# Causal attention with three score slots in place of four, and a PSUM bank of its own for turned reciprocals and weighted sums

## The chip, the cores and the metric

The kernel runs on one core of a Trainium2 chip. The metric is the device time of one execution in microseconds (us): from before the first instruction to after the last. Engines are named as the profile names them: PE is TensorE (matrix multiplies, PEld its weight loads), DVE is VectorE, ACT is ScalarE, POOL is GpSimd, SP is SyncE, which here only issues DMAs. Each has its own instruction stream and runs it in order; they meet at semaphores. PSUM is the small memory that PE writes and DVE and ACT read. The program allots it in eight banks of 512 float32 columns.

## The reference, cut to what matters

The program is a stack of four blocks (cross attention, windowed attention with feed forward, cross attention, experts). The change touches only the first attention of the first block, which is a self attention of 2 batches, 1024 tokens, 16 heads of 32 channels:

```python
q = jnp.einsum('bsc,hcd->bhsd', xn, wq)
k = jnp.einsum('btc,hcd->bhtd', yn, wk)
v = jnp.einsum('btc,hcd->bhtd', yn, wv)
a = jax.nn.softmax(jnp.einsum('bhsd,bhtd->bhst', q, k) * D ** (-0.5), axis=-1)
if causal:
    s, t = (a.shape[-2], a.shape[-1])
    mask = (jnp.arange(t)[None, :] > jnp.arange(s)[:, None]).astype(a.dtype)
    a = a * mask
o = jnp.einsum('bhst,bhtd->bhsd', a, v)
```

The mask keeps keys later than the query and is applied after the softmax. So the softmax runs over all 1024 keys, and only the blocks on and above the diagonal are weighted with the values.

## The kernel before

The work is cut in units. A unit is 128 query rows of one head against all 1024 keys; there are 256. Four heads make a quad, and the units run quad by quad (8 quads), in a quad by block of 128 queries (8 tiles), in a tile by head (4 units). `place(n)` gives the quad, the tile within it and the head of unit n. The number of key blocks that a unit keeps is `blocks(n)`: 8 in the first tile of a quad, 7 in the second, down to 1 in the last. This text calls it T, and a tile "T=7" when its units keep 7 blocks. One quad is thus 32 units.

A unit goes through six steps, each a function of the source:

- `score(n)` on PE: two matmuls of 512 columns write the 1024 scores into a slot, two PSUM banks, one a half.
- `row_max(n)` on DVE: the negated row maximum over the whole slot.
- `exponent(n)` on ACT: the exponential of the whole slot into `prob`, with the row sum.
- `turn(n)` on PE: T transposes of 128x128 from `prob` back into the same slot. With T above 4 they lie in both halves, else in half 0 alone.
- `evacuate(n)` on DVE and ACT: copies of the turned blocks to `probT`. `evac_parts(n)` deals them: with T=8 DVE takes half 0 and ACT half 1, with T=7 to 5 ACT takes half 0 and DVE half 1, with T of 4 and less one engine takes all, DVE for even heads and ACT for odd.
- POOL masks the diagonal block.

Once per tile, after its four units: `inverse` (DVE, reciprocals of the row sums), a broadcast on POOL, `turn_inverses` (PE, one transpose), `inverses` (ACT, copy to `rT`), `weigh` (PE, 4T matmuls with a column group each, shown by the profile as 8T instructions), and `output` (DVE, the product of the weighted sums with `rT`).

Nothing but the order in which these calls are written sets the order of the work. PE's is `turn(n)`, then once per tile `turn_inverses` and `weigh`, then `score(n + 3)`. DVE's is `row_max(n + 2)`, `evacuate(n)`, and once per tile `output`. ACT's is `exponent(n + 1)`, `evacuate(n)`, and once per tile `inverses`. The slots rotate: unit n uses slot n % 4, so `score(n + 3)` writes the slot of unit n - 1 and waits for that unit's evacuation, each half for the part that lies in it. Four slots fill all eight banks, so the turned reciprocals and the weighted sums of a tile have to borrow a slot (`home` says which), and the score that comes next into that slot waits for `rT` or for `output`.

The functions and lines that the change and the prediction touch:

## Time and profile before

| | us |
|---|---|
| median of 3 runs | 2074.62 (2074.13 to 2076.19) |
| span of the profiled execution, first to last instruction | 2082.0 |
| PE, DVE, ACT, POOL busy over the span | 1797.5, 1276.7, 1038.0, 698.8 |
| this attention: first score to last output | 109.4 to 564.1 |
| granted TensorE clock, mean over the span | 0.953 |

The profiled execution has no time of its own apart from its span; the span is 7.4 us above the median of the runs. Busy shares are means over the whole program. What one stage waits for is read from rows of that stage. A row of the timeline gives start, duration, engine, line and what it writes and reads, and in brackets how long the engine had been idle and which instruction ended that.

### The profile page before, as it was taken

Reading aid. Unit: us, or ns where it says so; the run is one execution under the profiler, and the core shown is the slowest. Engines: PE = TensorE matmul, PEld = TensorE weight load, DVE = VectorE, ACT = ScalarE, POOL = GpSimd, SP = SyncE. Lnnn points to the kernel's source line nnn. Section 1 sums busy time; section 2 is a strip of 40 time slices with the busy share of each in tenths; the row PEclk is TensorE's granted clock in tenths of the full one; section 3 lists DMA queues with packets and bytes.
Section 4 is the critical chain, followed back from the end, with each engine's and each line's share of the span. In section 5 each row is a group of like instructions: output and inputs, shape, how many; then the busy total and the mean of one; then the engine's idle time right before and its main releaser. Section 6 shows DMA issues by size and latency. Waiting matters only on the chain. (4 is left out here: it accounts for less than half of the span.)

```text
span 2082.0 us, 32325 instructions
## 1 busy us (share of the span) xinstructions
PE 1797.5 (86%) x11428; PEld 1190.9 (57%) x11428; DVE 1276.7 (61%) x2721; ACT 1038.0 (50%) x2198; POOL 698.8 (34%) x1001
## 2 busy tenths in 40 slices
PE   6988888888799897998899989999998998871895
PEld 3455555555566565766566655556666554550795
DVE  5478888898733485233788863258888344977112
ACT  3488888888722264121676741147675211540222
POOL 0022223232333343242465641125565112450322
PEclk9999999999999998999999999999999999995898
DMA  3441111110000100020000002010000000046595
GB/s 117 157 129 42 42 42 42 42 42 1 1 1 0 54 8 1 0 62 26 19 6 5 3 6 66 0 44 1 6 6 6 20 0 16 1 135 152 173 309 168
DMA packets 104896, 101.71 MB, mean 49 GB/s; under 512 B 34896, under 2 KB 88480, under 8 KB 104608
## 3 DMA queue, kind: packets, MB, share of 16 engines
q1 hardware_dynamic: 101664, 95.31, 15.4%
q0 software_dynamic: 3072, 4.34, 1.1%
q8 instruction: 92, 1.51, 0.3%
q14 instruction: 68, 0.56, 0.1%
HBM read 80.60 MB, written 16.92 MB: 47 GB/s over the span
## 5 line engine op out<-in xcount | busy, mean ns | idle before, releaser
L586 DVE TENSOR_REDUCE negmax<-sps 128x1 f32<-128x1024 f32 x256 | 308.3, 1215 | 36.4 <-PE sps L531 31.1
L630 ACT ACTIVATE prob<-sps,negmax 128x1024 f32<-128x1024 f32 x256 | 287.6, 1124 | 22.1 <-DVE negmax L586 18.3
L540 PE MATMUL sps<-ident,prob 128*128 128x128 f32 x1152 | 177.6, 282 | 57.6 <-ACT prob L630 56.6
L540 PEld LDWEIGHTS sps<-ident,prob 128*128 128x128 f32 x1152 | 134.0, 143 | 142.5 <-ACT prob L630 123.3
L1504 POOL TENSOR_TENSOR la_pr<-la_pr,la_ri 128x512 f32<-128x512 f32 x128 | 157.3, 1257 | 159.5 <-DVE la_ri L1567 159.5
L675 POOL TENSOR_TENSOR probT<-probT,after 128x128 f32<-128x128 f32 x256 | 117.0, 457 | 267.8 <-DVE probT L594 192.2
L1754 ACT ACTIVATE la_pr<-la_pr,la_nx 128x256 f32<-128x256 f32 x256 | 126.4, 494 | 127.4 <-DVE la_nx L1608 127.4
L531 PE MATMUL sps<-ks,qs 128*128 128x512 f16 x512 | 162.6, 393 | 10.6 <-DVE ores L606 4.4
L1939 PE MATMUL la_bs<-lf_zT,lfw 128*128 128x512 f32 x352 | 153.0, 594 | 0.0
L1514 POOL TENSOR_TENSOR la_qs<-la_qn,ores 128x256 f32<-128x256 f32 x128 | 113.9, 921 | 89.3 <-DVE la_qn L1621 89.3
L639 ACT COPY probT<-sps 128x512 f32<-128x512 f32 (+1 forms) x192 | 101.9, 531 | 40.4 <-PE sps L540 40.4
L1939 PEld LDWEIGHTS la_bs<-lf_zT,lfw 128*128 128x128 f32 x352 | 66.4, 190 | 82.5 <-issue 82.3
L1881 PE MATMUL la_bqk<-ores,la_hT 128*128 128x512 f32 x224 | 104.3, 608 | 0.0
L1948 PE MATMUL la_bqk<-lfw,lf_hT 128*128 128x256 f32 (+1 forms) x384 | 95.4, 392 | 2.3 <-DVE lf_hT L1664 2.3
L1608 DVE CUSTOM_DVE_ANT_0 la_pr<-la_bs,la_mf 128x256 f32<-128x256 f32 x256 | 90.7, 419 | 10.6 <-PE la_bs L1898 10.5
L1664 DVE SCALAR_TENSOR_TENSOR lf_hT<-la_bs,lfb,lf_gl 128x512 f32<-128x512 f32 (+1 forms) x48 | 35.9, 749 | 94.8 <-ACT lf_gl L1782 92.8
L1782 ACT ACTIVATE lf_gl<-la_bs,lfb 128x512 f32<-128x512 f32 x40 | 27.5, 687 | 132.2 <-PE la_bs L1939 132.2
L1824 PE MATMUL la_bs<-ident,la_pr 128*128 128x128 f32 x512 | 74.0, 292 | 22.2 <-POOL la_pr L1504 22.2
L594 DVE COPY probT<-sps 128x512 f32<-128x512 f32 (+3 forms) x192 | 91.7, 478 | 1.3 <-PE sps L540 1.3
L1824 PEld LDWEIGHTS la_bs<-ident,la_pr 128*128 128x128 f32 x512 | 61.6, 149 | 46.8 <-POOL la_pr L1504 34.3
L1948 PEld LDWEIGHTS la_bqk<-lfw,lf_hT 128*128 128x128 f32 (+1 forms) x384 | 68.3, 189 | 29.8 <-issue 18.4
L563 PE MATMUL sps<-probT,vres 128*32 128x128 f32 x2304 | 78.7, 281 | 0.3 <-POOL probT L675 0.3
(375 smaller groups left out, 3742.3 us busy)
## 6 DMA issues: line engine op xcount, KB each, us to landing
w1e<-in_fc_T SPq DMA_DIRECT2D x16, 1024.0 KB, 5.7
w2e<-in_fc_T SPq DMA_DIRECT2D x16, 1024.0 KB, 8.9
qs<-q_parts SPq DMA_DIRECT2D x128, 64.0 KB, 1.9
ks<-k_parts SPq DMA_DIRECT2D x128, 64.0 KB, 1.9
q_parts<-parts SPq DMA_DIRECT2D x8, 512.0 KB, 3.6
k_parts<-parts SPq DMA_DIRECT2D x8, 512.0 KB, 3.6
lfw<-in_L_ffn_w SPq DMA_DIRECT2D x6, 640.0 KB
ores<-in_L_ffn_wqkv SPq DMA_DIRECT2D x2, 1536.0 KB, 6.5
```

Source lines behind the costliest of these rows:

```text
L531: mm = pe.matmul(slots[n % 4][:, half * 512:(half + 1) * 512], qs[:, buf, i * P:(i + 1) * P], ks[:, buf, half * 512:(half + 1) * 512], sta ...
L540: mm = pe.transpose(slots[n % 4][:, at * P:(at + 1) * P], prob[:, n % 3, t * P:(t + 1) * P], ident[:])
L586: dve.tensor_reduce(negmax[:, n % 4:n % 4 + 1], slots[n % 4][:], X, ALU.max, negate=True).then_inc(s.max_done, 1)
L630: act.activation(prob[:, n % 3, :], slots[n % 4][:], ACT.Exp, bias=negmax[:, n % 4:n % 4 + 1], accum_out=rowsum[:, tile % 2, n % QUAD:n % ...
L675: pool.tensor_tensor(blk, blk, after[:], ALU.mult).then_inc(s.masked, 1)
L1504: ins = pool.tensor_tensor(prob[:, h:h + 2, :], prob[:, h:h + 2, :], rinv[:, h:h + 2].unsqueeze(2).to_broadcast([P, 2, 2 * P]), ALU.mult)
L1514: pool.tensor_tensor(qs[:, q * HL:(q + 1) * HL, a * 32:(a + 1) * 32], qn[:, q * HL:(q + 1) * HL, (1 - a) * 32:(2 - a) * 32], sinr[:, t % T ...
L1754: ins = act.activation(prob[:, h, :], prob[:, h, :], ACT.Exp, scale=-1.0, bias=nmax[:, h:h + 1], accum_out=rsum[:, h:h + 1])
L1824: mm = pe.transpose(bs[:, half * 1024 + n * 256 + w * P:half * 1024 + n * 256 + (w + 1) * P], prob[:, h, w * P:(w + 1) * P], ident[:])
L1881: mm = pe.matmul(raw(t)[:, n * INNER:(n + 1) * INNER], shifted_rows(t, k), wqkv[:, k, n, :], start=(k == 0), stop=(k == KD - 1))
L1939: mm = pe.matmul(dst, w1[:, k, at:at + P], zT[:, k, :], start=(k == 0), stop=(k == KD - 1))
L1948: mm = pe.matmul(p3[j // 2][:, j % 2, :], uT[0:n, f, j * P:(j + 1) * P], w2[0:n, f, :], start=(f == 0), stop=(f == NF - 1))
```

## The change

PSUM is divided anew: three score slots (six banks) and one bank `wps`, whose first 128 columns take the turned reciprocals and whose second 128 the weighted sums. One bank stays free. `home` and the waits that went with the borrowed slot are gone. On PE, `score` now runs two units ahead and stands in front of `turn(n)`; `turn_inverses` comes ahead of `turn` too; and `weigh` comes one unit later, ahead of that unit's `turn`. `output` on DVE is one unit later. On ACT, `inverses` goes ahead of `evacuate`. `row_max(n + 2)` ahead of `evacuate(n)` on DVE stays as it was. Unit n now uses slot n % 3, so `score(n + 2)` writes the slot of unit n - 1.

PE before, from unit 2 to unit 7; `sps` with its number is a slot, x8 are eight transposes, and the number of blocks tells the tile:

```order
L540 MATMUL sps2<-ident,prob 128x128 x8
L531 MATMUL sps1<-ks,qs 128x512 x2
L540 MATMUL sps3<-ident,prob 128x128 x8
L531 MATMUL sps2<-ks,qs 128x512 x2
L540 MATMUL sps0<-ident,prob 128x128 x7
L547 MATMUL sps3<-ident,rwide 128x128
L563 MATMUL sps3<-probT,vres 32x128 x32
L531 MATMUL sps3<-ks,qs 128x512 x2
L540 MATMUL sps1<-ident,prob 128x128 x7
L531 MATMUL sps0<-ks,qs 128x512 x2
L540 MATMUL sps2<-ident,prob 128x128 x7
L531 MATMUL sps1<-ks,qs 128x512 x2
```

PE after the change, at the same place (line 524 is `score`, 533 `turn`, 540 `turn_inverses`, 556 `weigh`):

```order
L524 MATMUL sps1<-ks,qs 128x512 x2
L533 MATMUL sps2<-ident,prob 128x128 x8
L524 MATMUL sps2<-ks,qs 128x512 x2
L533 MATMUL sps0<-ident,prob 128x128 x8
L524 MATMUL sps0<-ks,qs 128x512 x2
L540 MATMUL wps<-ident,rwide 128x128
L533 MATMUL sps1<-ident,prob 128x128 x7
L524 MATMUL sps1<-ks,qs 128x512 x2
L556 MATMUL wps<-probT,vres 32x128 x32
L533 MATMUL sps2<-ident,prob 128x128 x7
L524 MATMUL sps2<-ks,qs 128x512 x2
L533 MATMUL sps0<-ident,prob 128x128 x7
```

The score that refills the slot of unit n - 1 stood behind `turn(n)`; it stands ahead of it now. `weigh` stood between a `turn` and a `score`; it stands between a `score` and a `turn`.

DVE before, the same units (586 is `row_max`, 594 `evacuate`, 600 `inverse`, 606 `output`):

```order
L594 COPY probT<-sps1 128x512
L586 TENSOR_REDUCE negmax<-sps0 128x1
L594 COPY probT<-sps2 128x512
L586 TENSOR_REDUCE negmax<-sps1 128x1
L600 RECIPROCAL rinv<-rowsum 128x4
L594 COPY probT<-sps3 128x512
L586 TENSOR_REDUCE negmax<-sps2 128x1
L594 COPY probT<-sps0 128x384
L606 TENSOR_TENSOR ores<-sps3,rT 128x128
L586 TENSOR_REDUCE negmax<-sps3 128x1
```

DVE after the change (580 `row_max`, 588 `evacuate`, 594 `inverse`, 600 `output`):

```order
L588 COPY probT<-sps1 128x512
L580 TENSOR_REDUCE negmax<-sps1 128x1
L588 COPY probT<-sps2 128x512
L580 TENSOR_REDUCE negmax<-sps2 128x1
L594 RECIPROCAL rinv<-rowsum 128x4
L588 COPY probT<-sps0 128x512
L580 TENSOR_REDUCE negmax<-sps0 128x1
L588 COPY probT<-sps1 128x384
L580 TENSOR_REDUCE negmax<-sps1 128x1
L588 COPY probT<-sps2 128x384
```

The order of kinds is the same but for `output`. The slots differ: before, the copy out of one slot was followed by the maximum of another that had been filled a unit earlier; now it is followed by the maximum of the very slot that was just copied out.

The diff, cut to its core:

```diff
@@ -470,7 +470,9 @@
             rT = sb("rT", [P, 2, P], F32, c)
-            slots = [ps(f"sps{i}", [P, N], c) for i in range(4)]
+            NS = 3
+            slots = [ps(f"sps{i}", [P, N], c) for i in range(NS)]
+            wps = ps("wps", [P, 2, P], c)
 
             def place(n):
@@ -491,11 +493,6 @@
             def evacuated(who, n):
 
                 return sum(part[0] == who for m in range(n + 1) for part in evac_parts(m))
-
-            def home(tile):
-
-                nxt = tile * QUAD + QUAD
-                return 0 if nxt < UNITS and blocks(nxt) <= 4 else QUAD - 1
 
             s = signals("a1a", "@cleared @after_ready @scores @max_done @exp_done @masked "
                         "@turned @evac_act @evac_dve @rinv_done @widened @r_turned @rT_done @pv_done @out_done @next_in")
@@ -518,17 +515,13 @@
                         if i == 0:
                             pe.wait_ge(landed[buf], 128 * (quad // 2 + 1))
                         for half in range(2):
-                            if n >= 4:
-                                for who, lo, _ in evac_parts(n - 4):
+                            if n >= NS:
+                                if half == 0:
+                                    pe.wait_ge(s.exp_done, n - NS + 1)
+                                for who, lo, _ in evac_parts(n - NS):
                                     if lo // 4 == half:
-                                        pe.wait_ge(s.evac_act if who == "act" else s.evac_dve, evacuated(who, n - 4))
-                            if half == 0 and j == QUAD - 1 and n > QUAD:
-                                pe.wait_ge(s.rT_done, n // QUAD)
-                            if half == 1 and j == QUAD - 1 and n > QUAD and home(n // QUAD - 1) == QUAD - 1:
-                                pe.wait_ge(s.out_done, n // QUAD)
-                            if half == 1 and j == 0 and n > QUAD and home(n // QUAD - 2) == 0:
-                                pe.wait_ge(s.out_done, n // QUAD - 1)
-                            mm = pe.matmul(slots[n % 4][:, half * 512:(half + 1) * 512], qs[:, buf, i * P:(i + 1) * P],
+                                        pe.wait_ge(s.evac_act if who == "act" else s.evac_dve, evacuated(who, n - NS))
+                            mm = pe.matmul(slots[n % NS][:, half * 512:(half + 1) * 512], qs[:, buf, i * P:(i + 1) * P],
                                            ks[:, buf, half * 512:(half + 1) * 512], start=True, stop=True)
                         mm.then_inc(s.scores, 1)
@@ -537,21 +530,21 @@
                         pe.wait_ge(s.exp_done, n + 1)
                         for at in range(total):
                             t = i + 1 + at if at < total - 1 else i
-                            mm = pe.transpose(slots[n % 4][:, at * P:(at + 1) * P], prob[:, n % 3, t * P:(t + 1) * P], ident[:])
+                            mm = pe.transpose(slots[n % NS][:, at * P:(at + 1) * P], prob[:, n % 3, t * P:(t + 1) * P], ident[:])
                         mm.then_inc(s.turned, 1)
 
                     def turn_inverses(tile):
-                        who, last = evac_parts(tile * QUAD + QUAD - 1)[0][0], tile * QUAD + QUAD - 1
-                        pe.wait_ge(s.evac_act if who == "act" else s.evac_dve, evacuated(who, last))
+                        if tile > 0:
+                            pe.wait_ge(s.out_done, tile)
                         pe.wait_ge(s.widened, tile + 1)
-                        pe.transpose(slots[QUAD - 1][:, 0:P], rwide[:, tile % 2, :, :].rearrange("p h d -> p (h d)"),
+                        pe.transpose(wps[:, 0, :], rwide[:, tile % 2, :, :].rearrange("p h d -> p (h d)"),
                                      ident[:]).then_inc(s.r_turned, 1)
 
                     def weigh(tile):
                         last = tile * QUAD + QUAD - 1
                         quad, i, _ = place(last)
                         total = blocks(last)
-                        acc = slots[home(tile)]
+                        pe.wait_ge(s.rT_done, tile + 1)
                         for who, sem in (("act", s.evac_act), ("dve", s.evac_dve)):
                             if evacuated(who, last):
                                 pe.wait_ge(sem, evacuated(who, last))
@@ -560,20 +553,21 @@
                             if t == i:
                                 pe.wait_ge(s.masked, last + 1)
                             for j in range(QUAD):
-                                mm = pe.matmul(acc[j * D1:(j + 1) * D1, 512:512 + P], vres[:, quad * QUAD + j, t, :],
+                                mm = pe.matmul(wps[j * D1:(j + 1) * D1, 1, :], vres[:, quad * QUAD + j, t, :],
                                                probT[:, (tile * QUAD + j) % 6, at * P:(at + 1) * P],
                                                start=(at == 0), stop=(at == total - 1))
                         mm.then_inc(s.pv_done, 1)
 
-                    for n in range(3):
+                    for n in range(2):
                         score(n)
                     for n in range(UNITS):
-                        turn(n)
+                        if n + 2 < UNITS:
+                            score(n + 2)
                         if n % QUAD == 0 and n > 0:
                             turn_inverses(n // QUAD - 1)
+                        if n % QUAD == 1 and n > QUAD:
                             weigh(n // QUAD - 1)
-                        if n + 3 < UNITS:
-                            score(n + 3)
+                        turn(n)
                     turn_inverses(UNITS // QUAD - 1)
                     weigh(UNITS // QUAD - 1)
...
@@ -603,7 +597,7 @@
                         quad, i, _ = place(tile * QUAD)
                         dve.wait_ge(s.pv_done, tile + 1)
                         dve.wait_ge(s.rT_done, tile + 1)
-                        dve.tensor_tensor(ores[:, quad, i * P:(i + 1) * P], slots[home(tile)][:, 512:512 + P], rT[:, tile % 2, :],
+                        dve.tensor_tensor(ores[:, quad, i * P:(i + 1) * P], wps[:, 1, :], rT[:, tile % 2, :],
                                           ALU.mult).then_inc(s.out_done, 1)
 
                     row_max(0)
@@ -614,7 +608,7 @@
                         if n % QUAD == QUAD - 1:
                             inverse(n // QUAD)
                         evacuate(n)
-                        if n % QUAD == 0 and n > 0:
+                        if n % QUAD == 1 and n > QUAD:
                             output(n // QUAD - 1)
                     output(UNITS // QUAD - 1)
...
@@ -636,21 +630,21 @@
                                 act.wait_ge(s.turned, n + 1)
                                 if n >= 6:
                                     act.wait_ge(s.pv_done, (n - 6) // QUAD + 1)
-                                act.copy(probT[:, n % 6, lo * P:hi * P], slots[n % 4][:, lo * P:hi * P]).then_inc(s.evac_act, 1)
+                                act.copy(probT[:, n % 6, lo * P:hi * P], slots[n % NS][:, lo * P:hi * P]).then_inc(s.evac_act, 1)
 
                     def inverses(tile):
                         act.wait_ge(s.r_turned, tile + 1)
                         if tile >= 2:
                             act.wait_ge(s.out_done, tile - 1)
-                        act.copy(rT[:, tile % 2, :], slots[QUAD - 1][:, 0:P]).then_inc(s.rT_done, 1)
+                        act.copy(rT[:, tile % 2, :], wps[:, 0, :]).then_inc(s.rT_done, 1)
 
                     exponent(0)
                     for n in range(UNITS):
                         if n + 1 < UNITS:
                             exponent(n + 1)
-                        evacuate(n)
                         if n % QUAD == 0 and n > 0:
                             inverses(n // QUAD - 1)
+                        evacuate(n)
                     inverses(UNITS // QUAD - 1)
 
                 @block.gpsimd
```

Left out are three places where `slots[n % 4]` became `slots[n % NS]` and nothing else.

## Rows read from the trace of the kernel before

**Rows 1.** Windows, this attention: length, busy of PE, PEld, DVE, ACT, POOL, clock, DMA.

```profile
109.00:563.00 454.00, 375.86 (x4024) 241.18 (x4024) 394.85 (x575) 391.54 (x768) 134.24 (x322) 0.97 0.16 43
```

**Rows 2.** Groups of this attention by form: busy us, mean ns | idle before, releasers.

```profile
L586 DVE TENSOR_REDUCE negmax<-sps 128x1 f32<-128x1024 f32 x256 | 308.3, 1215 | 36.4 <-PE sps L531 31.1 <-ACT prob L630 5.2
L630 ACT ACTIVATE prob<-sps,negmax 128x1024 f32<-128x1024 f32 x256 | 287.6, 1124 | 22.1 <-DVE negmax L586 18.3 <-PE sps L540 1.8
...
L639 ACT COPY probT<-sps 128x512 f32<-128x512 f32 x144 | 84.2, 585 | 34.5 <-PE sps L540 34.5
...
L594 DVE COPY probT<-sps 128x512 f32<-128x512 f32 x48 | 32.5, 678 | 1.3 <-PE sps L540 1.3
L594 DVE COPY probT<-sps 128x384 f32<-128x384 f32 x48 | 26.1, 544 | 0.0
...
L594 DVE COPY probT<-sps 128x256 f32<-128x256 f32 x48 | 19.7, 411 | 0.0
...
L594 DVE COPY probT<-sps 128x128 f32<-128x128 f32 x48 | 13.3, 277 | 0.0
...
L639 ACT COPY probT<-sps 128x384 f32<-128x384 f32 x16 | 7.6, 474 | 2.3 <-PE sps L540 2.3
L639 ACT COPY probT<-sps 128x256 f32<-128x256 f32 x16 | 5.9, 368 | 1.2 <-PE sps L540 1.2
L639 ACT COPY probT<-sps 128x128 f32<-128x128 f32 x16 | 4.2, 264 | 2.3 <-PE sps L540 2.3
```

**Rows 3.** Timeline of all engines, first units of a T=7 tile: start, us, instruction.

```profile
233.72 1.95 PE L563 MATMUL sps<-probT,vres 128*32 128x128 f32 x64
...
235.60 0.39 PE L531 MATMUL sps<-ks,qs 128*128 128x512 f16 x1
235.74 0.29 DVE L606 TENSOR_TENSOR ores<-sps,rT 128x128 f32<-128x128 f32 x1 [0.74 <-PE sps L563]
...
236.18 0.38 PE L531 MATMUL sps<-ks,qs 128*128 128x512 f16 x1 [0.18 <-DVE ores L606]
...
236.39 0.93 PE L540 MATMUL sps<-ident,prob 128*128 128x128 f32 x7
236.59 1.23 DVE L586 TENSOR_REDUCE negmax<-sps 128x1 f32<-128x1024 f32 x1 [0.56 <-PE sps L531]
...
237.15 0.59 PE L531 MATMUL sps<-ks,qs 128*128 128x512 f16 x2
237.35 0.59 ACT L639 COPY probT<-sps 128x512 f32<-128x512 f32 x1 [1.58 <-PE sps L540]
...
237.58 0.93 PE L540 MATMUL sps<-ident,prob 128*128 128x128 f32 x7
...
238.19 1.22 DVE L586 TENSOR_REDUCE negmax<-sps 128x1 f32<-128x1024 f32 x1
...
239.32 0.55 DVE L594 COPY probT<-sps 128x384 f32<-128x384 f32 x1
...
239.79 1.22 DVE L586 TENSOR_REDUCE negmax<-sps 128x1 f32<-128x1024 f32 x1
```

**Rows 4.** Timeline of PE, where a tile T=4 is weighed and T=3 turned.

```profile
263.49 1.08 PE L563 MATMUL sps<-probT,vres 128*32 128x128 f32 x32
264.50 0.61 PE L531 MATMUL sps<-ks,qs 128*128 128x512 f16 x2
264.94 0.49 PE L540 MATMUL sps<-ident,prob 128*128 128x128 f32 x3
```

**Rows 5.** Line 547, once per tile: durations in ns, first and last start in us.

```profile
L547 PE MATMUL sps<-ident,rwide x64: 272/300/448, 120.1 to 562.4; 128*128 128x128 f32 x64
```

**Rows 6.** Windows of PE at a fall of the clock: length, busy, clock, DMA.

```profile
277.00:279.00 2.00, 2.00 (x7) 0.50 0.05 11
```

**Rows 7.** Timeline of PE in that stretch.

```profile
276.94 1.04 PE L531 MATMUL sps<-ks,qs 128*128 128x512 f16 x2
277.77 0.42 PE L540 MATMUL sps<-ident,prob 128*128 128x128 f32 x1
```

More of the change, by code:

```diff
@@ L585, in row_max @@
                             dve.wait_ge(s.exp_done, n - 3)
-                        dve.tensor_reduce(negmax[:, n % 4:n % 4 + 1], slots[n % 4][:], X, ALU.max, negate=True).then_inc(s.max_done, 1)
+                        dve.tensor_reduce(negmax[:, n % 4:n % 4 + 1], slots[n % NS][:], X, ALU.max, negate=True).then_inc(s.max_done, 1)
                     def evacuate(n):
@@ L593, in evacuate @@
                                     dve.wait_ge(s.pv_done, (n - 6) // QUAD + 1)
-                                dve.tensor_copy(probT[:, n % 6, lo * P:hi * P], slots[n % 4][:, lo * P:hi * P]).then_inc(s.evac_dve, 1)
+                                dve.tensor_copy(probT[:, n % 6, lo * P:hi * P], slots[n % NS][:, lo * P:hi * P]).then_inc(s.evac_dve, 1)
                     def inverse(tile):
@@ L629, in exponent @@
                             act.wait_ge(s.rinv_done, tile - 1)
-                        act.activation(prob[:, n % 3, :], slots[n % 4][:], ACT.Exp, bias=negmax[:, n % 4:n % 4 + 1],
+                        act.activation(prob[:, n % 3, :], slots[n % NS][:], ACT.Exp, bias=negmax[:, n % 4:n % 4 + 1],
                                        accum_out=rowsum[:, tile % 2, n % QUAD:n % QUAD + 1]).then_inc(s.exp_done, 1)
```

## The prediction, on record before the changed kernel ran

> **What bounds the stage now.** I read the windows of the stage first, then its groups, then the timeline of a few units. Over 454 us PE, DVE and ACT were busy 83, 87 and 86% [rows 1], so none alone is the answer. The groups show whole-slot passes: a row maximum of 1215 ns and an exponential of 1124 ns for each unit, then copies of 264 to 678 ns [rows 2]. The timeline shows two regimes. Inside a tile DVE is never idle: maximum at 238.19, copy at 239.32 (1.13 later), next maximum at 239.79, a period of 1.60 us [rows 3]. Once per tile the chain breaks: `weigh` holds PE from 233.72 to 235.60, the score behind it waits for `output`, and DVE idles 0.74 and 0.56 us and ACT 1.58 us [rows 3]. Line 547 runs once per tile, from 120.1 to 562.4 over 63 intervals [rows 5]: 7.02 us a tile, 56.2 us a quad of eight tiles.
>
> **What the row of 236.59 says.** In those 0.56 us DVE waited for a score whose second half waited for DVE's own product: the product ends at 236.03, the matmul starts at 236.18 (0.15), takes 0.38, and the maximum starts 0.03 after its end [rows 3]. That is the price of asking PE to refill a slot that DVE has only just left, and then waiting for it. Before, it is paid once per tile.
>
> **What the change adds.** `score(n+2)` needs unit n-1 evacuated. DVE does `evacuate(n-1)`, then `row_max(n+2)`, which reads that score, and only then `evacuate(n)`. So the 0.56 us is now in every unit, and in series with both DVE passes. Before, `score(n+3)` needed the same evacuation, but DVE's next maximum was that of n+2, already scored: one unit of slack. That slack is gone, and no engine has work to put there, since `turn(n)` too stands behind the score on PE. A count of slots alone would hide this: the loop through one slot (refill, maximum, exponential, turn, copy, with handovers) is about 0.15+0.38+0.03+1.22+0.03+1.12+0.15+0.93+0.03+0.55, some 4.6 us for three units, under the old 1.60 each [rows 2, 3].
>
> Period of a unit after the change, in us, from rows at full clock:
> - T=7, 6, 5 (DVE copies half 1): 0.56 + 1.13 + copy 0.55, 0.41, 0.28 [rows 2, 3] = 2.24, 2.10, 1.97. ACT, which copies half 0, ends earlier: with T=7 the turn is issued 0.21 after the score's second half, which begins 0.41 before the maximum, and ends 0.73 after the maximum's start; ACT's copy ends at 1.34, and it may be 1.47 (DVE's copy ends at 1.68, and half 0 wants 0.21 ahead of half 1). So a later turn shows from 0.13 us on (0.10 and 0.08 for T=6 and 5).
> - T=8 (DVE copies half 0): both score matmuls follow, 0.59 in place of 0.38 [rows 3]: 0.15 + 0.59 + 0.03 + 1.13 + 0.68 = 2.58. The turn ends at 0.84 and is wanted at 1.10, so it has 0.26 of slack.
> - T=4 to 1, two units together, since DVE copies the even one and ACT the odd: maximum 1.13, DVE copy, 0.15, score issue 0.43 (237.15 to 237.58), turn, 0.03, ACT copy, 0.15 + 0.59 + 0.03 to the next maximum [rows 3]. A turn of 7 blocks takes 0.93 and of 3 0.49 [rows 3, 4], so 0.11 a block, and 0.60, 0.38, 0.27 for 4, 2, 1. With the copies of [rows 2]: 4.37, 4.02, 3.66. With T=1 the exponential is later than the turn: 1.22 + 0.03 + 1.12 + 0.26 + 0.77 = 3.40.
>
> Four units a tile, T=8 down to 1: 10.32 + 8.96 + 8.40 + 7.88 + 8.74 + 8.04 + 7.32 + 6.80 = 66.5 us a quad.
>
> **Once per tile.** `weigh` holds PE 1.88 us for 64 instructions and 1.01 for 32 (263.49 to 264.50) [rows 3, 4]; between them on a line: 1.66, 1.45, 1.23, 0.79, 0.58, 0.36 for 56, 48, 40, 24, 16, 8. It now delays `turn(4k+1)`, and with it the copy, the next score and the next maximum, less the slack above. The tile of T units pays for T+1 blocks: T=7 1.75, T=6 1.56, T=5 1.37, T=4 1.23, T=3 1.01, T=2 0.79, T=1 0.50, T=8 0.10; sum 8.3. The serial part of the old boundary, PE's, is thus not removed but moved. What does go are the waits for the borrowed slot. `output` now fits into DVE's 0.56 us and costs nothing; if that cover went it would cost 0.2 a tile. The reciprocal ahead of a copy and the transposed reciprocals (0.30, [rows 5]) ahead of a turn add an estimated 0.7 a quad. ACT's copy of them ends during the turn: nothing. `turn_inverses`' wait for `output` and `weigh`'s for `rT` are for work ended a unit earlier or more. SP's loads wait for scores two quads back and have a longer quad to land in: nothing.
>
> **Sum.** 66.5 + 8.3 + 0.7 = 75.5 us a quad against 56.2; times 63/8 quads, +152 us.
>
> **The clock.** PE will be less busy, so its clock matters. From 277 to 279 it was at 1.2 GHz, half [rows 6]; a score pair took 1.04 there in place of 0.59, a turn of one block 0.42 in place of 0.27 [rows 7]. It fell in the lightest tiles, where PE had little to do in a unit. The stage's mean of 0.97 [rows 1] is 6% of it at 1.2 GHz, 3.4 us a quad: one fall of some two units a quad. For a pair of T=1 units at the low level the turn's path decides: 1.13+0.28+0.15+0.86+0.42+0.03+0.26+0.15+1.04+0.03 = 4.35, +0.95 over 3.40. The price is 0 if the falls stay as many, and +9.4 a quad if all tiles of T=4 to 1 run so (2.7, 2.5, 2.3 and 1.9 by the same path, with 0.22 a block), +75 in all. I take three falls a quad where there was one, two more of two units each: +15, nearer the low end since that is where the rows are.
>
> The Trainium skill has a rule that speaks against this change ("TensorE: Matmul & The Clock Gate", "A second HAM failure mode: psum-queue depth-cycling"): small idle gaps between groups of matmuls, repeated with each turn of the PSUM banks, make the clock swing between its levels. The rows bear it out only at the light tiles. By it the sum would be that of rival A.
>
> The profiled execution spans 2082.0, 7.4 above the median of the runs; differences carry over. 2074.6 + 152 + 15 = **2242 us** (its profile 2249).
>
> **Rivals.**
> - A, the low clock over all light tiles: 2074.6 + 152 + 75 = 2302. For it: PE now waits for a slot in every unit and is busy 0.43 + 0.60 us of 2.19 with T=4, 0.43 + 0.27 of 1.70 with T=1. Against: at the low level the same work fills more of the time, as the full 2.00 of 2.00 us of [rows 6] shows, and the clock came back after it. Chance 0.09.
> - B, half of the new wait is hidden: some order that I read as serial overlaps, say because PE's loss to `weigh` is caught up inside the tile. Half of 152: 2151, with 2100 to 2200 as its own range. Against: every link is an in-order engine. Chance 0.07; 0.01 of it for no change at all, if DVE's maximum did not wait and the loop of 4.6 us per three units were the only bound.
> - C, the other side: the borrowed slot was the real cost, and its own bank frees DVE's 0.74 + 0.56 us per tile: 63 x 1.30 = 82, so 1993. For it: these waits [rows 3], and the 31.1 us that the maxima waited for scores [rows 2]. It decides if `score(n+2)` is complete before DVE ends `evacuate(n)`; that takes a slot free a unit earlier, which three slots don't give. Chance 0.03.
> - The sum as above: 0.81.
>
> So faster by over 0.2% (about what a measurement of this kernel tells from none) 0.03, within it 0.01, slower 0.96. The range, 2195 to 2305, holds the sum with clock costs from 0 to 75 us, below that an error of 0.03 us in each unit's handover (8 us) or of three or four us a quad in `weigh`.
>
> **What would show it.** In the profile after: DVE idle of about 0.56 us before nearly each maximum in T=7 to 5 and 0.77 in the others, released by the score line, some 145 us in all where it was 31; maxima 2.24 us apart with T=7 and 2.58 with T=8; ACT's busy share of the stage down from 86 to about 65%; the stage some 605 us long; everything behind it unchanged. If idle before the maximum stays near 36 us, the serial chain is wrong; if the spacing holds but the stage is longer, the clock is the rest. If maxima in T=7 stay 1.6 us apart, the forecast is wrong altogether.

## The result, and the profile after

| | before | after |
|---|---|---|
| median, us | 2075.4 (4 runs) | 2306.12 (2298.2 to 2313.94, 4 runs) |
| span of the profiled execution, us | 2082.0 | 2296.4 |
| first to last row maximum of this attention, us | 448.8 | 678.7 |
| granted clock, mean of the span | 0.953 | 0.913 |

The ratio is 1.1094 (95% interval 1.1046 to 1.1142): slower, as forecast, but by 231 us where 167 were forecast. By the medians the time lies 64 us above the forecast and 1 us above the top of the range; by the ratio (1.1094 of 2075.4 is 2302) it lies just inside it.

It is in this attention: between its first and last row maximum 229.9 us came on. The medians are 230.7 apart; that these two agree so closely is partly luck. Behind the last maximum, where the instructions are the same, the profile of before took 1522.8 us and that of after 1507.4. The two spans are therefore only 214.4 apart. This stretch moves by some 15 us without any change: e1, below, took 1522.6 in it and e11 1507.4. Line 586 of before and line 580 of after are the same instruction (columns: line, engine, operation, tile, count: shortest/median/longest ns, first and last start in us; the last field is the shape of the commonest form):

```profile
L586 DVE TENSOR_REDUCE negmax<-sps x256: 1192/1215/1227, 110.4 to 559.2; 128x1 f32<-128x1024 f32 x128
```
```profile
L580 DVE TENSOR_REDUCE negmax<-sps x256: 1212/1224/1226, 110.3 to 789.0; 128x1 f32<-128x1024 f32 x128
```

The windows of after, with the columns of [rows 1]: the whole stage, a stretch of the first quad from T=8 into T=4, and two stretches at a low clock.

```profile
109.00:794.00 685.00, 454.44 (x4032) 267.94 (x4032) 412.43 (x576) 410.62 (x768) 133.48 (x322) 0.81 0.11 29
112.00:160.00 48.00, 31.22 (x364) 21.82 (x364) 31.73 (x45) 33.10 (x61) 9.25 (x22) 1.00 0.44 128
169.00:197.00 28.00, 18.55 (x85) 7.26 (x83) 14.51 (x20) 14.53 (x29) 5.06 (x13) 0.50 0.11 28
254.00:296.00 42.00, 30.37 (x156) 14.79 (x156) 21.39 (x29) 20.03 (x39) 7.12 (x17) 0.50 0.19 50
```

DVE's and ACT's work is what it was, within 5% (412 and 411 us; 395 and 392 in [rows 1]), but it is now 60% of the stage and not 87%. So they wait. The second thing to see is the granted clock, the third number from the end of a row: it is 0.81 for the stage, where [rows 1] had 0.97. The groups say what the waits are for (busy us, mean ns | idle before, releasers):

```profile
L580 DVE TENSOR_REDUCE negmax<-sps 128x1 f32<-128x1024 f32 x256 | 313.3, 1224 | 226.2 <-PE sps L524 226.0
L624 ACT ACTIVATE prob<-sps,negmax 128x1024 f32<-128x1024 f32 x256 | 285.7, 1116 | 72.7 <-DVE negmax L580 69.1
L533 PE MATMUL sps<-ident,prob 128*128 128x128 f32 x1152 | 203.4, 311 | 2.1 <-ACT prob L624 2.1
L524 PE MATMUL sps<-ks,qs 128*128 128x512 f16 x512 | 191.9, 460 | 228.2 <-DVE probT L588 113.6 <-ACT probT L633 111.5 <-PEq L42 3.1
```

The maxima waited 226 us for scores, where [rows 2] had 31, and the scores waited 228 us for copies. Each waits for the other: that is the serial chain of the prediction. It is there in every unit, T=7 at full clock (the timeline, from DVE and PE; in brackets the idle time before and what ended it):

```profile
125.40 1.95 PE L556 MATMUL wps<-probT,vres 128*32 128x128 f32 x64
125.50 1.22 DVE L580 TENSOR_REDUCE negmax<-sps 128x1 f32<-128x1024 f32 x1 [0.54 <-PE sps L524]
127.28 0.98 PE L533 MATMUL sps<-ident,prob 128*128 128x128 f32 x7
128.30 0.56 DVE L588 COPY probT<-sps 128x384 f32<-128x384 f32 x1 [1.57 <-PE sps L533]
...
129.66 1.23 DVE L580 TENSOR_REDUCE negmax<-sps 128x1 f32<-128x1024 f32 x1 [0.60 <-PE sps L524]
130.80 0.55 DVE L588 COPY probT<-sps 128x384 f32<-128x384 f32 x1
131.84 1.22 DVE L580 TENSOR_REDUCE negmax<-sps 128x1 f32<-128x1024 f32 x1 [0.48 <-PE sps L524]
133.06 0.53 DVE L588 COPY probT<-sps 128x384 f32<-128x384 f32 x1
134.07 1.22 DVE L580 TENSOR_REDUCE negmax<-sps 128x1 f32<-128x1024 f32 x1 [0.48 <-PE sps L524]
```

Maxima start 2.18 and 2.23 us apart, with 0.48 of idle time before them. Where `weigh` stands ahead of the turn they are 4.16 apart: DVE idles 1.57 us before its copy, since the turn behind 1.95 us of `weigh` began late. And so it goes at the low clock, T=2: 

```profile
270.21 1.01 PE L524 MATMUL sps<-ks,qs 128*128 128x512 f16 x2 [0.55 <-ACT probT L633]
271.01 0.63 PE L533 MATMUL sps<-ident,prob 128*128 128x128 f32 x2
271.26 1.22 DVE L580 TENSOR_REDUCE negmax<-sps 128x1 f32<-128x1024 f32 x1 [1.86 <-PE sps L524]
272.96 1.01 PE L524 MATMUL sps<-ks,qs 128*128 128x512 f16 x2 [1.31 <-DVE probT L588]
```

A score takes 1.01 us where it took 0.59, and DVE waits 1.86 us for it.

**Lengths of the tiles.** In us, second quad, from the starts of the maxima: from the third unit of a tile to the third of the next, since the maximum runs two units ahead. "Full clock" is a run with a small extra matmul, told below, in which the clock did not fall there.

| T | 8 | 7 | 6 | 5 | 4 | 3 | 2 | 1 |
|---|---|---|---|---|---|---|---|---|
| before | 8.02 | 8.13 | 7.49 | 7.00 | 6.74 | 6.42 | 6.07 | 5.86 |
| predicted, full clock, without the 0.7 a quad | 10.42 | 10.71 | 9.96 | 9.25 | 9.97 | 9.05 | 8.11 | 7.30 |
| after, full clock (e11) | 11.37 | 10.80 | 10.10 | 9.39 | 10.17 | 9.25 | 8.33 | 7.49 |
| after | 13.42 | 10.80 | 10.09 | 9.39 | 11.42 | 12.46 | 11.12 | 9.79 |

The tiles of the last row that are longer than those above ran at 1.2 GHz in whole or in part. The quads of after differ: T=8 took 13.3 to 14.4 us from the second quad on, its first 6.2 to 10.7 us at 1.2 GHz, and 10.70 in the first quad, at full clock; T=4 took 10.2 to 11.4, T=3 10.3 to 12.5, T=2 8.3 to 11.1. T=7 to 5 kept their full-clock length in every quad. In the profile of after the clock was low in twelve stretches, 266 us in all: three of 3.4 us and nine of 13.7 to 47.8. One of the two longest, from 248.7 to 296.5, begins in T=4 of the second quad, covers T=3 to 1 and reaches through most of the next quad's T=8. Before had seven falls, 3.4 us each.

### The profile page after: what moved, and what is told of

It is laid out like the page before. It is cut to its first block and busy times, and to the rows that moved or that the text cites. A ratio compares the mean times of both kernels' runs of the same rounds, so it can differ in the third digit from the quotient of the medians.

```text
span 2296.4 us, 32477 instructions
## 1 busy us (share of the span) xinstructions
PE 1862.3 (81%) x11428; PEld 1209.0 (53%) x11428; DVE 1294.3 (56%) x2721; ACT 1056.6 (46%) x2198; POOL 697.3 (30%) x1001
## 5 line engine op out<-in xcount | busy, mean ns | idle before, releaser
L580 DVE TENSOR_REDUCE negmax<-sps 128x1 f32<-128x1024 f32 x256 | 313.3, 1224 | 226.2 <-PE sps L524 226.0
L524 PE MATMUL sps<-ks,qs 128*128 128x512 f16 x512 | 191.9, 460 | 228.2 <-DVE probT L588 113.6
L533 PE MATMUL sps<-ident,prob 128*128 128x128 f32 x1152 | 203.4, 311 | 2.1 <-ACT prob L624 2.1
L524 PEld LDWEIGHTS sps<-ks,qs 128*128 128x128 f16 x512 | 38.4, 99 | 309.6 <-issue 262.6
L533 PEld LDWEIGHTS sps<-ident,prob 128*128 128x128 f32 x1152 | 159.3, 161 | 52.9 <-issue 33.5
L1602 DVE CUSTOM_DVE_ANT_0 la_pr<-la_bs,la_mf 128x256 f32<-128x256 f32 x256 | 90.7, 419 | 10.6 <-PE la_bs L1892 10.5
L556 PE MATMUL wps<-probT,vres 128*32 128x128 f32 x2304 | 87.8, 302 | 0.4 <-ACT rT L639 0.4
```

The costliest lines, as they stand in the source:

```text
L524: mm = pe.matmul(slots[n % NS][:, half * 512:(half + 1) * 512], qs[:, buf, i * P:(i + 1) * P], ks[:, buf, half * 512:(half + 1) * 512], st ...
L533: mm = pe.transpose(slots[n % NS][:, at * P:(at + 1) * P], prob[:, n % 3, t * P:(t + 1) * P], ident[:])
L580: dve.tensor_reduce(negmax[:, n % 4:n % 4 + 1], slots[n % NS][:], X, ALU.max, negate=True).then_inc(s.max_done, 1)
```

## The experiments

PE's order in a unit of after is: score two ahead, turned reciprocals, `weigh` (once per tile), turn. All the kernels are after with the edits shown, but for e7, which is before with one. "Stage" is the time from the first to the last row maximum: 448.8 before, 678.7 after.

### Does the clock hold the missing 64 us?

**e1.** PE gets work of no use in the bank that stayed free, so that it is busy while it waits.

```diff
+            fil = ps("fil", [P, 512], c)
...
                         turn(n)
+                        pe.matmul(fil[:], ident[:], vres[:, 0:2, :, :].rearrange("p a b c -> p (a b c)"), start=True, stop=True)
```

> The changed kernel with one more matmul of 512 float32 columns behind every turn, into the free eighth bank; nobody reads it. It fills PE's idle time (0.44 us where PE waits 0.55 to 1.6 us for a slot). Theory 'serial chain at full clock plus low clock': PE stays at 2.4 GHz in the whole stage, every tile takes its full-clock length (10.8, 10.1, 9.4, 10.3 us for T=7 to 4 as before, T=3 to 1 and 8 near 9.4, 8.6, 7.7 and 10.6 instead of 12.4, 11.2, 10.1 and 13), the stage shrinks from 669 to about 606 us and the time is 2243. Rival 'the clock is no cause, only a mark of a PE that waits': the clock may rise but the tiles keep their lengths, 2306 or more by the added PE work.

2246.51 us, ratio 1.0799 (1.0739 to 1.086). The stage took 616.3 us, its clock was 1.00:

```profile
109.00:732.00 623.00, 578.44 (x4544) 306.67 (x4544) 411.83 (x576) 409.69 (x768) 133.59 (x322) 1.00 0.12 32
```

So 60 us went by giving PE more to do. But the filler, 1.02 us of PE (two instructions in the trace) where 0.44 had been expected, sticks out in the light tiles: T=1 took 7.92 us, and 7.49 in e11, with half the filler.

**e11.** The same with 256 columns (0.60 us), to take that out.

```diff
                         turn(n)
+                        pe.matmul(fil[:, 0:256], ident[:], vres[:, 0:1, :, :].rearrange("p a b c -> p (a b c)"), start=True, stop=True)
```

> The changed kernel with the filler of 256 columns in every unit, half as long as in the first filler run, so that it sticks out of no wait. Theory: the full clock alone, without a cost of the filler: 10.6, 10.8, 10.1, 9.4, 10.2, 9.2, 8.2, 7.5 us for T=8 down to 1, a stage of 598 us, 8 to 10 us less than with 512 columns; about 2225 to 2235. Rival 'the filler of 512 cost nothing': 607 and 2246.

2228.66 us, 1.0725 (1.0675 to 1.0774); stage 613.5 us.

```profile
109.00:725.00 616.00, 488.21 (x4532) 304.99 (x4530) 410.53 (x574) 408.64 (x765) 132.22 (x319) 0.99 0.11 32
```

This is the run that splits the stage's 229.9 us: 613.5 - 448.8 = 164.7 for the serial chain and `weigh`, 678.7 - 613.5 = 65.2 for the clock. The filler itself adds nothing that the tiles show: T=7 to 5 have the same lengths with and without it, and so have T=4 (10.17) and T=2 (8.33) in those quads of after that kept the clock. By tiles, 47 of the 65 us lie in T=3 to 1, 4 in T=4, and 16 in T=8 of the second to eighth quad; e11 ran low itself for its first 10 us, which takes 2 off.

The medians are 77 us apart, 12 more than the stages; the spans of the two profiled executions are 65.9 apart, so I lay nothing on these 12. The time came as expected, but the stage is 15 us above the 598 expected: T=8 took 11.37 us and not 10.6, in each quad, and the eight lengths of the expectation add up to some 608 by themselves.

**e10.** The 256 columns only in units with `blocks(n) <= 4`. It asks whether T=8 runs low on its own or because it is entered so.

```diff
                         turn(n)
+                        if blocks(n) <= 4:
+                            pe.matmul(fil[:, 0:256], ident[:], vres[:, 0:1, :, :].rearrange("p a b c -> p (a b c)"), start=True, stop=True)
```

> The changed kernel with a matmul of 256 float32 columns behind the turn, in the tiles T=4 to 1 alone; nobody reads it. It asks where the falls of the clock begin. Theory 'they begin in the light tiles and T=8 only inherits them': all tiles at 2.4 GHz, T=8 at 10.6 us where it took 13.4 to 14.4, the stage near 600 us, the time near 2230. Rival 'T=8, with PE half idle, falls by itself': T=8 still takes 12 to 14 us and shows 1.2 GHz, the stage near 625 and the time near 2250.

2237.47 us, 1.0754 (1.0701 to 1.0806); stage 617.0. Two windows, the first quad's T=8 and T=7, which no filled tile stands ahead of, and the second quad's T=8:

```profile
114.00:131.00 17.00, 13.61 (x93) 9.66 (x95) 8.84 (x10) 7.35 (x15) 2.11 (x5) 0.50 0.70 225
190.00:201.00 11.00, 6.39 (x45) 3.87 (x44) 8.01 (x11) 7.30 (x16) 2.47 (x6) 1.00 0.52 142
```

Same units, same code: behind filled tiles, in seven quads, T=8 stayed at 2.4 GHz and took 11.37 us. In the first quad the clock fell inside T=8, at 113.9 us, and stayed at 1.2 GHz for 17.1 us, into T=7; T=8 took 13.62, where it took 10.70 in after at full clock. So most of what T=8 lost in after began in the light tiles, and a fall there is paid for in the next quad too. But a fall in T=8 needs no light tile ahead of it: this one had none, PE had idled 3.07 us before its first scores and waited in each unit after. The stage is 17 us above the 600 expected: 5.5 us are the first quad's T=8 and T=7 over their full-clock lengths, and 5.4 the 0.8 us that each later T=8 took above the expected 10.6. The expectation's "all tiles at 2.4 GHz" is right for seven quads of eight.

### Which part of the change is the chain?

**e5 and e6.** Without the once-per-tile work, with three slots (e5) and with four (e6). The cut shows PE's part of e5 and what e6 adds; left out of it are the same calls on DVE and ACT, and the waits on `weigh`, which became waits on POOL's mask.

```diff
-                        if n % QUAD == 0 and n > 0:
-                            turn_inverses(n // QUAD - 1)
-                        if n % QUAD == 1 and n > QUAD:
-                            weigh(n // QUAD - 1)
...
```
```diff
-            NS = 3
+            NS = 4
```

> The changed kernel without anything that is done once per tile on the weighted sums: the turn of the reciprocals, weigh and output are left out, and the attention's output is set to zero instead. Three slots. Theory 'serial chain, because a slot is refilled only one unit ahead of its use': maxima stay 2.58, 2.24, 2.10, 1.97 us apart for T=8 to 5 at full clock, 66.5 us a quad, 532 in all, plus some 60 us of low clock since PE has still less to do; about 2220. Rival 'weigh and its waits are the cause': units at 1.6 us and about 2010.

> The same with four slots and nothing else changed: same order on every engine, scores ahead of turns by two units. Theory: score(n+2) now needs unit n-2 evacuated, DVE never waits for a slot it has just left, and the units take what DVE and ACT need: 1.73, 1.60, 1.59, 1.59, 1.43, 1.36, 1.30, 1.23 us for T=8 down to 1, 47.3 us a quad, a stage of about 385 us and a time near 2005. Rival 'the order on PE (scores ahead of turns) is what costs': as slow as with three slots, near 2220.

e5 2243.77 us (before on that chip 2072.33), stage 611.8; e6 2001.28, stage 373.5, one run each. The two programs differ in the number of slots alone, and 242 us lie between. DVE with T=7, first three slots, then four:

```profile
123.30 1.23 DVE L574 TENSOR_REDUCE negmax<-sps 128x1 f32<-128x1024 f32 x1 [0.78 <-PE sps L524]
124.44 0.55 DVE L582 COPY probT<-sps 128x384 f32<-128x384 f32 x1
125.47 1.23 DVE L574 TENSOR_REDUCE negmax<-sps 128x1 f32<-128x1024 f32 x1 [0.48 <-PE sps L524]
```
```profile
119.77 1.22 DVE L573 TENSOR_REDUCE negmax<-sps 128x1 f32<-128x1024 f32 x1
120.91 0.55 DVE L581 COPY probT<-sps 128x384 f32<-128x384 f32 x1
121.37 1.21 DVE L573 TENSOR_REDUCE negmax<-sps 128x1 f32<-128x1024 f32 x1
```

With four slots the second maximum follows the copy at once, 1.60 us after the first; with three it waits 0.48 for its score, 2.17 after. A tile of T=7 took 8.75 and 6.45 us: four units of 0.57 more. All 256 maxima of e6 waited 12.0 us in sum.

Not all of the 242 us is the refill's. In e5 the clock of the stage was 0.71, lower than in after, and in e6 it fell for 3.4 us only:

```profile
109.00:723.00 614.00, 384.77 (x1663) 215.35 (x1663) 395.71 (x510) 401.19 (x701) 132.53 (x319) 0.71 0.12 32
```

Taking `weigh` away took work from PE, and part of what it saved was lost again to the clock (T=4 to 1 at low clock took 11.3, 10.4, 9.5 and 8.6 us, at full clock T=8 to 5 10.69, 8.75, 8.22 and 7.68). With the expectation's 532 us for the stage at full clock, an estimate, the clock cost some 80 us of e5 where 60 were expected, which is most of the 24 us by which it missed; the slot itself is then worth some 160 us of the 238 between the stages.

**e9.** e1, and with T=8 too DVE copies half 1, so that the score's first half need not wait for it.

```diff
-                low, high = ("dve", "act") if total == TPB else ("act", "dve")
+                low, high = ("act", "dve")
```

> The changed kernel with the filler of 512 columns, and for T=8 the halves dealt the other way: ACT copies half 0 and DVE half 1. Theory: only one score matmul then follows DVE's copy, the maxima of T=8 come 0.15+0.38+0.03+1.13+0.68 = 2.37 us apart in place of 2.58, and the tile T=8 takes 9.75 us in place of 10.59; the other tiles keep 10.80, 10.10, 9.43, 10.34. Rival 'the halves do not matter, the score counts as one': 10.59.

2235.58 us, stage 609.6. Maxima of T=8 start 2.37 us apart where after had 2.60:

```profile
195.47 1.23 DVE L582 TENSOR_REDUCE negmax<-sps 128x1 f32<-128x1024 f32 x1 [0.48 <-PE sps L525]
196.70 0.66 DVE L590 COPY probT<-sps 128x512 f32<-128x512 f32 x1
197.84 1.23 DVE L582 TENSOR_REDUCE negmax<-sps 128x1 f32<-128x1024 f32 x1 [0.48 <-PE sps L525]
```

So the wait is 0.48 behind one score matmul and 0.78 behind two (the prediction had 0.56 and 0.77). It is the refill, by its path. The whole tile took 10.39 us where 9.75 was expected; the gain against e1, which took 11.19, is the expected 0.8, and the 0.6 that both are too long lies in the tile's first units (see below).

### What does `weigh` cost where it stands?

**e3.** `turn(n)` ahead of `weigh`, else after.

```diff
+                        turn(n)
                         if n % QUAD == 1 and n > QUAD:
                             weigh(n // QUAD - 1)
-                        turn(n)
```

> The changed kernel with weigh behind the turn of the same unit instead of ahead of it. Theory: weigh then runs while PE waits for the copy, so only what sticks out of that wait is paid: a tile of T=7 falls from 10.8 to about 9.9, T=6 from 10.1 to 9.2, T=5 from 9.4 to 8.5, T=4 from 10.3 to 9.5; 5 to 6 us a quad, about 2262. Rival 'weigh is paid in full wherever it stands, since PE is the bound': 2306.

2251.12 us, 1.0828 (1.0775 to 1.0881), 55 less than after; stage 626.8, clock still 0.81:

```profile
109.00:742.00 633.00, 445.31 (x4032) 277.91 (x4032) 414.74 (x575) 414.61 (x769) 133.79 (x322) 0.81 0.11 31
```

The weighed unit of T=7 was 3.19 us long and not 4.16. An unweighed one takes 2.2, so `weigh` cost 1.0 us there and not 2.0: it then delays the next score instead of the turn, and half of it fits into PE's wait. Half of what `weigh` costs in after is thus the cost of its place.

**e8.** e3, with the 256-column filler in each unit that has no `weigh`.

```diff
+                        turn(n)
                         if n % QUAD == 1 and n > QUAD:
                             weigh(n // QUAD - 1)
-                        turn(n)
+                        else:
+                            pe.matmul(fil[:, 0:256], ident[:], vres[:, 0:1, :, :].rearrange("p a b c -> p (a b c)"), start=True, stop=True)
```

> The changed kernel with weigh behind the turn and, in the three other units of a tile, one matmul of 256 float32 columns behind the turn into the free bank, read by nobody. Theory: the two gains add, since one is PE time moved into a wait and the other the clock: tiles 9.8, 9.1, 8.5, 9.4 as in the run with weigh behind, T=3, 2, 1 and 8 at about 8.6, 8.1, 7.6, 10.4 instead of up to 10.5, 9.9, 9.4, 12.9; a stage of about 565 us and 2200. Rival 'the filler does not hold the clock when it is half as long': 2250.

2179.88 us, 1.0537 (1.0467 to 1.0607); stage 561.8 us, the shortest of the three-slot kernels that do all the work.

```profile
109.00:675.00 566.00, 446.74 (x4409) 290.36 (x4409) 409.82 (x575) 412.78 (x767) 133.62 (x321) 1.00 0.13 35
```

It is still 113 us above before's stage, with the refill in every unit and `weigh` largely out of the way.

### Can another order hide the refill?

**e2.** PE turns first: turned reciprocals, `turn(n)`, `weigh`, `score(n + 2)`.

```diff
-                        if n + 2 < UNITS:
-                            score(n + 2)
                         if n % QUAD == 0 and n > 0:
                             turn_inverses(n // QUAD - 1)
+                        turn(n)
                         if n % QUAD == 1 and n > QUAD:
                             weigh(n // QUAD - 1)
-                        turn(n)
+                        if n + 2 < UNITS:
+                            score(n + 2)
```

**e4.** DVE copies first.

```diff
-                        if n + 2 < UNITS:
-                            row_max(n + 2)
                         if n % QUAD == QUAD - 1:
                             inverse(n // QUAD)
                         evacuate(n)
...
+                        if n + 2 < UNITS:
+                            row_max(n + 2)
```

**e12.** e11 with e4's order on DVE, and ACT's copies ahead of its exponential:

```diff
-                        if n + 1 < UNITS:
-                            exponent(n + 1)
                         if n % QUAD == 0 and n > 0:
                             inverses(n // QUAD - 1)
                         evacuate(n)
+                        if n + 1 < UNITS:
+                            exponent(n + 1)
```

> The changed kernel with PE's order of before: turn(n), weigh, then score(n+2); three slots and the own bank stay. Theory 'serial chain through DVE': T=8 to 5 keep maxima 2.58, 2.24, 2.10, 1.97 us apart, since copy, score, maximum, copy is still a loop of one unit; the light tiles lose the turn from their path (pairs 3.75, 3.62, 3.51, 3.41) and weigh costs some 1.1 us a tile instead of up to 1.75: about 2247. Rival 'PE's order is the cause': maxima go back to 1.6 us apart and the time to about 2090.

> The changed kernel with DVE's order turned: evacuate(n) ahead of row_max(n+2). It breaks the loop of one unit (copy, score, maximum, copy) and puts a loop of two units in its place (maximum, exponential, turn, copy: 1.22+0.03+1.12+0.15+0.98+0.03+0.47 = 4.0 us for T=7). Theory 'serial chain through DVE's order': units at 2.12, 2.00, 1.88, 1.77 for T=8 to 5 in place of 2.58, 2.24, 2.10, 1.97, weigh still paid in full, about 2245. Rival 'the slot count alone sets the pace whatever the order on DVE': no change, 2306, maxima 2.24 us apart.

> The changed kernel with both copies put first: on DVE evacuate(n) ahead of row_max(n+2), on ACT evacuate(n) ahead of exponent(n+1); with the filler of 256 columns, so that the clock stays full. It follows the run with DVE's order turned alone, in which a loop of two units of 4.95 us stood in T=7: maximum, exponential, ACT's copy of the unit before (queued behind that exponential), score, turn, copy. Theory 'that queueing on ACT is what ate the gain': with ACT's order turned too the loop is maximum, exponential, turn, copy, 4.0 us for two units, so T=7 units come 2.0 us apart on average where weigh does not stand, the tiles T=8 to 1 take some 9.0, 9.9, 9.2, 8.6, 8.9, 8.1, 7.5, 6.8 us, the stage 540 us, the time about 2155. Rival 'the order of the copies makes no difference with three slots': T=7 pairs of 4.4 us or more, tiles as with the filler alone, 2228.

All three missed. e2 2326.26 us, 1.1191 (1.1137 to 1.1244); e4 2345.8, 1.1316 (1.1258 to 1.1374); e12 2270.0 (before there 2074.78), stage 643.3.

Two of the three also ran at a low clock, e2 first, then e4:

```profile
109.00:818.00 709.00, 483.43 (x4022) 304.23 (x4020) 403.55 (x572) 401.22 (x764) 132.29 (x318) 0.79 0.10 28
109.00:828.00 719.00, 472.58 (x4020) 296.12 (x4018) 403.26 (x572) 402.34 (x762) 133.36 (x317) 0.79 0.10 27
```

The clock was low for 314 us of e2 and 297 of e4, in stretches of 3.4 to 20.5 us, and no run holds it up there; so how much of their times is the order and how much the clock is not shown. For e12 it is: at a clock of 0.99 it took 30 us more in the stage than e11.

In e2 the spacing of 2.17 inside a tile stood, and the boundary grew: DVE waits once for the score behind a turn that waits for POOL's reciprocals, and once for that behind `weigh`. (The `weigh` of these rows took 2.44 us for 56 instructions, partly at 1.2 GHz; in e11 it took 1.74.)

```profile
139.23 1.23 DVE L580 TENSOR_REDUCE negmax<-sps 128x1 f32<-128x1024 f32 x1 [1.77 <-PE sps L524]
140.40 2.44 PE L556 MATMUL wps<-probT,vres 128*32 128x128 f32 x56
142.77 0.60 PE L524 MATMUL sps<-ks,qs 128*128 128x512 f16 x2
143.41 1.23 DVE L580 TENSOR_REDUCE negmax<-sps 128x1 f32<-128x1024 f32 x1 [2.63 <-PE sps L524]
```

In e4 I had followed DVE and not seen that ACT's copy of unit n+1 is queued behind ACT's exponential of n+2, which waits for the maximum:

```profile
127.87 1.22 DVE L580 TENSOR_REDUCE negmax<-sps 128x1 f32<-128x1024 f32 x1
129.12 1.11 ACT L624 ACTIVATE prob<-sps,negmax 128x1024 f32<-128x1024 f32 x1 [1.14 <-DVE negmax L580]
130.23 0.58 ACT L633 COPY probT<-sps 128x512 f32<-128x512 f32 x1
130.95 0.59 PE L524 MATMUL sps<-ks,qs 128*128 128x512 f16 x2 [1.46 <-ACT probT L633]
131.38 0.93 PE L533 MATMUL sps<-ident,prob 128*128 128x128 f32 x7
132.34 0.56 DVE L588 COPY probT<-sps 128x384 f32<-128x384 f32 x1 [1.04 <-PE sps L533]
132.82 1.22 DVE L580 TENSOR_REDUCE negmax<-sps 128x1 f32<-128x1024 f32 x1
```

A loop over two units of 4.95 us, in place of two of 2.18. e12 moves ACT's exponential out of that loop and meets the next one: exponential of a unit, its turn, ACT's copy of it, exponential of the next.

```profile
136.69 1.12 ACT L626 ACTIVATE prob<-sps,negmax 128x1024 f32<-128x1024 f32 x1
137.96 0.87 PE L534 MATMUL sps<-ident,prob 128*128 128x128 f32 x6 [0.32 <-ACT prob L626]
138.87 0.59 ACT L635 COPY probT<-sps 128x512 f32<-128x512 f32 x1 [0.81 <-PE sps L534]
139.35 1.12 ACT L626 ACTIVATE prob<-sps,negmax 128x1024 f32<-128x1024 f32 x1
```

These are 2.66 us apart here with T=6 and 2.77 with T=7 (1.12 + 0.15 + 0.98 + 0.03 + 0.48). By tiles, e12 against e11: T=7, 6 and 5 took 12.22, 11.56 and 11.44 us in place of 10.80, 10.10 and 9.39, but T=4, 3 and 2 took 9.82, 8.69 and 7.56 in place of 10.17, 9.25 and 8.33. So the turned orders lengthen the loop in the heavy tiles and shorten it in three of the light ones. No order tried brought three slots near four; an order chosen by T was not tried.

### Does the filler help the kernel before?

**e7.** Before, with a matmul of no use into the upper half of a slot that only light units leave free:

```diff
                         if n + 3 < UNITS:
                             score(n + 3)
+                        if n % QUAD == 2 and blocks(n) <= 3:
+                            pe.matmul(slots[n % 4][:, 512:1024], ident[:], vres[:, 0:2, :, :].rearrange("p a b c -> p (a b c)"), start=True, stop=True)
```

> The kernel before, with one matmul of 512 float32 columns in the tiles T=3 to 1, ahead of the turn of the tile's last unit, where PE waits 1.04 to 1.29 us for an exponential; it goes to the half of a slot that holds nothing any more. Theory 'a short fall costs 0.7 to 1.15 us each in this stage, and PE work in idle time prevents it': no fall in the stage, all T=8, T=2 and T=1 tiles at 8.02, 6.07 and 5.86, the stage 5 us shorter (444 from the first to the last maximum, it was 448.8), about 2070. Rival 'the falls cost nothing here': 448.8 and no change. The change of the median will be close to what can be told; the stage's length in the trace decides.

2063.47 us against 2077.59, ratio 0.994 (0.9917 to 0.9964): 0.6% below before. Stage 443.6 us where before had 448.8, no fall in it but that of its first 2 us:

```profile
109.00:558.00 449.00, 388.51 (x4080) 245.57 (x4080) 394.56 (x575) 390.85 (x768) 133.70 (x322) 1.00 0.16 44
```

Each quad's tiles now took 8.02, 8.13, 7.49, 7.00, 6.74, 6.42, 6.07 and 5.85 us. The stage gives 5.2 of the 14 us. That the rest belongs to the filler is not shown: behind the stage, where nothing was changed, e7's profile took 1506.9 us and before's 1522.8, but those of after and e11 took 1507.4 there too.

## Why the prediction was right and where it was wrong

- **The refill chain in every unit: right, in place and size.** 2.24 us forecast with T=7, 2.18 to 2.24 measured; 2.58 with T=8, 2.60; 4.37 for a pair of T=4 and 3.40 for a pair of T=1, 4.39 and 3.40 in e8. e6 shows that it hangs on the number of slots: with a fourth the wait is gone.
- **The boundary: right, a little small.** At full clock a quad took 76.9 us and 75.5 were forecast. `weigh` and the turned reciprocals together cost 2.05, 1.88 and 1.70 us a tile with T=7, 6 and 5 (e11's tiles less e5's at full clock), where 1.75, 1.56 and 1.37 were forecast for `weigh`; the units came out 0.05 us shorter each, so these tiles are only 0.1 us too long, and T=4 to 1 are 0.2 too long each. The largest miss is T=8, 11.37 against 10.42: its first units stand 3.26 and 2.85 us apart where 2.60 is the unit. There the turned reciprocals wait for POOL's broadcast, and DVE's copy for the turn behind them (e11, PE, then DVE):

```profile
190.57 0.30 PE L541 MATMUL wps<-ident,rwide 128*128 128x128 f32 x1 [0.65 <-POOL rwide L666]
191.78 0.69 DVE L590 COPY probT<-sps 128x512 f32<-128x512 f32 x1 [0.60 <-PE sps L534]
```

I had put 0.7 us for the reciprocals of the whole quad, and this one place takes nearly all of it. Together: 165 us and not 152.

- **Rival B and C: out.** Nothing of the wait was hidden, and the borrowed slot was not the cost: its DVE waits went and 226 us of others came, 177 at full clock (e11), where the forecast's sign was some 145.
- **The clock: the step that failed, by its size.** The sum took 15 us for it, three falls of two units a quad; 65 is what e11 against after gives. Two things had kept the term low. The first is the sentence that at the low level the same work fills more of the time, so that the clock comes back, read from [rows 6], where PE was busy for 2.00 us of 2.00. In after PE was busy for 18.55 us of 28 and for 30.37 of 42 at 1.2 GHz and it did not come back: at the low level the chain through DVE grew longer as well, so PE still waited in every unit. The second is a term put at nothing without a reason: even the dearest case priced T=4 to 1 alone. T=8 behind them was entered at the low level and lost 2 to 3 us in seven quads. The prices of a tile at 1.2 GHz were near, 2.5, 2.3 and 1.9 us for T=3, 2 and 1 against 3.2, 2.8 and 2.3 in the second quad. It was the number and the length of the falls that were wrong. Only the rows of a kernel without such waits could be read, and I let their two-unit falls stand for one that waits in every unit.
- **Rival A, with a chance of 0.09, is the nearest: 2302 against 2306.** Part of that is luck. Its 75 us were for T=4 to 1 at the low level throughout, and these tiles lost 51; T=8, which it left out, lost 14, and the chain's error of 13 came on top.

The Trainium skill ("TensorE: Matmul & The Clock Gate", "A second HAM failure mode: psum-queue depth-cycling") says of a kernel with bf16 matmuls that small idle gaps between its groups of matmuls, coming back as the PSUM banks go round, make the clock swing. This case's trace agrees for the light tiles: 0.81 granted over the stage where it was 0.97, and 0.99 when e11 put a matmul into the gaps. It does not agree everywhere: from 112 to 160 us, T=8 to 5 and part of T=4 in the first quad, PE waited for a slot in each unit too, was busy for 31.22 us of 48, and was granted 1.00. What the kernel before could not show was how long a fall lasts, and the price hung on that. What makes the clock fall or come back these runs do not isolate.

Chance and range: the range's upper end held rival A but no error of the chain beside it; 13 us of the chain and 65 of the clock came together.

## What to carry to other kernels

Follow the loop, not the count of buffers: where engine X must empty a slot, engine Y refill it and X then read it, the refill stands in X's time in every round unless one more slot lies between. Here one slot was worth 238 us of the stage (e5 against e6), some 160 of them by itself and the rest by the clock, an estimate. When a change makes PE wait in every round, price its clock over whole tiles, from the light ones on into those that follow, and try first whether a small matmul into a free bank holds the level; it gave 65 us of the stage here and 5 in the kernel before. Before an order is turned round, write down for every engine what is queued in front of each link, ACT's as well: three of my orders were longer loops in the heavy tiles than the one that they replaced, and two of them ran at a lower clock than the filled kernels besides.

## What the runs showed of the hardware that was not expected

- Once at 1.2 GHz, PE stayed there for up to 47.8 us; in two windows of such stretches it was busy for 66 and 72% of the time. In a window of 48 us at 2.4 GHz it was busy for 65%. So the busy share of a stretch did not tell its level here.
- Less work on PE saved nothing where the clock fell further: e5, without `weigh`, ran its stage at 0.71 and took 611.8 us, as long as e11 with all the work and a filler (613.5).
- The filler matmul of float32 shows as two instructions in the trace: 1.02 us of PE for 512 columns, 0.60 for 256, both at 2.4 GHz.
